# Two-layer expert routing in two equal halves, each with its own counts and slots, nine early tiles instead of eleven

## What is computed

```
x = x + 0.5 * ffn(layernorm(x), router, experts, shared)      # layer 1
x = x + attn(layernorm(x))                                    # test-time training, 1024 steps in order
x = x + 0.5 * ffn(layernorm(x), router, experts, shared)      # layer 2

def ffn(h):
    probs = softmax(h @ router.T)            # 8 experts
    p, i = top_k(probs, 2)
    w = p / sum(p)
    out = sum over k of w[k] * (relu(h @ fc[i[k]].T) ** 2 @ proj[i[k]].T)
    return out + relu(h @ shared_fc.T) ** 2 @ shared_proj.T
```

## Time and profile before

| what | us |
|---|---|
| median of 3 runs | 483.91 |
| lowest and highest run | 483.69, 485.36 |
| span of the profiled execution | 483.5 |
| PE busy in it | 433.4 (90%) |
| DVE busy | 280.3 (58%) |
| ACT busy | 244.4 (51%) |
| POOL busy | 242.4 (50%) |

### The profile page before, as it was taken

One profiled execution on the slowest core, in us unless ns is written; L12 is line 12 of the kernel. 1 busy time (PEld: TensorE's weight loads), 2 busy tenths in 40 slices (PEclk: granted clock), 3 DMA queues, 4 the chain that ended last, 5 costly groups with the idle time before them and its releaser, 6 DMA issues.

```text
span 483.5 us, 9868 instructions
## 1 busy us (share of the span) xinstructions
PE 433.4 (90%) x2875; PEld 356.7 (74%) x2875; DVE 280.3 (58%) x1031; ACT 244.4 (51%) x617; POOL 242.4 (50%) x371
## 2 busy tenths in 40 slices
PE   7899899999918889999999999989999699999940
PEld 5444599999903668999999999974644399999930
DVE  3836445555429657677777767754965245555514
ACT  2495255555510545655556555544597145555520
POOL 4367777445510344455555646542247767454530
PEclk9599999999976999999999999999799999999975
DMA  8981435100055300000000000000001417110028
GB/s 223 253 290 50 111 89 172 31 28 28 12 155 170 82 1 1 1 2 2 1 3 0 1 2 2 3 1 0 2 23 55 112 50 204 35 34 28 20 62 216
DMA packets 34513, 30.89 MB, mean 64 GB/s; under 512 B 3838, under 2 KB 30085, under 8 KB 34464
## 3 DMA queue, kind: packets, MB, share of 16 engines
q1 hardware_dynamic: 24608, 19.17, 14.8%
q0 software_dynamic: 4544, 8.47, 5.4%
q10 hardware_dynamic: 5312, 2.62, 2.1%
HBM read 15.55 MB, written 15.61 MB: 64 GB/s over the span
## 4 chain that ended last, share of the span: by engine, by line
PE 80%; DVE 5%; DMA 5%; POOL 4%; issue 3%; ACT 1%; ACTq 0%; DVEq 0%; SPq 0%; POOLq 0%
PE bank L1307 17%; PE bank L741 15%; PE bank L728 14%; PE bank L689 5%; PE bank L699 3%; PE bank L599 3%; POOL slots_dram L1436 3%; DMA stage<-y_dram 3%; PE bank L1101 2%; PE bank L716 2%; PE bank L1176 2%; PE bank L1139 1%; PE bank L1161 1%; PE bank L1205 1%; DVE stats L419 1%
## 5 line engine op out<-in xcount | busy, mean ns | idle before, releaser
L1693 DVE TENSOR_TENSOR sq<-bank,relu 128x512 f32<-128x512 f32 x86 | 59.4, 691 | 85.6 <-ACT relu L839 85.3
L1441 POOL DMA_INDIRECT y_dram<-y_out,stage x78 | 76.5, 981 | 60.8 <-ACT y_out L865 54.3
L741 PE MATMUL bank<-proj_w,sq 128*128 x624 | 86.4, 281 | 2.9 <-DVE sq L1693 2.9
L728 PE MATMUL bank<-tileT,tile_w 128*128 128x128 f32 x624 | 83.2, 277 | 0.1
L1436 POOL DMA_INDIRECT slots_dram<-rows,slots x64 | 63.0, 984 | 37.4 <-issue 15.5
L741 PEld LDWEIGHTS bank<-proj_w,sq 128*128 128x128 f32 x624 | 75.6, 191 | 6.5 <-issue 3.6
L839 ACT ACTIVATE relu<-bank 128x512 f32<-128x512 f32 x94 | 56.0, 596 | 47.5 <-PE bank L728 38.0
L728 PEld LDWEIGHTS bank<-tileT,tile_w 128*128 128x128 f32 x624 | 76.9, 194 | 0.4 <-ACT tileT L831 0.4
L865 ACT ACTIVATE y_out<-bank,stage 128x128 f32<-128x128 f32 x78 | 28.6, 367 | 33.3 <-PE bank L741 33.3
L1302 POOL TENSOR_TENSOR sq<-sq,last_rows 128x128 f32<-128x128 f32 x32 | 14.6, 456 | 53.6 <-DVE sq L1278 53.6
L689 PE MATMUL bank<-ln_t,fc_w 128*128 128x512 f32 x64 | 36.9, 678 | 0.0
(11 more groups left out here) (280 smaller groups left out, 1035.3 us busy)
## 6 DMA issues: line engine op xcount, KB each, us to landing
slots_dram<-pad SPq DMA_DIRECT2D x2, 2535.0 KB, 14.1
stage<-slots_dram SPq DMA_DIRECT2D x18, 260.0 KB, 4.7
fc_w<-experts SPq DMA_DIRECT2D x1, 2048.0 KB, 20.9
proj_w<-experts SPq DMA_DIRECT2D x1, 2048.0 KB, 23.8
stage<-y_dram SPq DMA_DIRECT2D x8, 256.0 KB, 5.5
stage<-y_dram ACTq DMA_DIRECT2D x8, 256.0 KB, 6.1
y_dram<-y_out,stage POOLq DMA_INDIRECT x78, 2.3
res<-x SPq DMA_DIRECT2D x4, 256.0 KB, 4.2
```

What stands on the lines that cost most here:

```text
L728: last = nc.tensor.matmul(bank[i % 2][:, f_cols], tile_w[:, i % 2, f_cols], tileT[:, (f * NQ + tile_q(i)) % 2, tile_cols(i)], start=True, ...
L741: last = nc.tensor.matmul(bank[4 + i % 2][:, 0:P], sq[:, i % 2, f_cols], proj_w[:, k, f_cols], start=j == 0, stop=j == FJ - 1)
L1441: nc.gpsimd.indirect_dma_start(y_dram.ap(), bass.IndirectOffsetOnAxis(tiles[:, t, P:P + 1].bitcast(U32), 0), y_out[:, t % YBUFS, :], None, ...
L1693: nc.vector.tensor_tensor(wide_of(i)[2], wide_of(i)[0][:], wide_of(i)[1], ALU.mult)\
```

## The change

`HALF` becomes 8 blocks, so 16 scatters belong to each half, and `EARLY` becomes 9 tiles. The whole of the routing is done once for each half: `choose` (two best experts, counts), `weigh` and `weights_made` (the two weights), then `first_slots` for the first half and `late_slots` for the second, whose counts take a second set of products on PE (`pe_counts(pe, f, 1)`). The second half's norms, its 1/sqrt (now on DVE, `late_scale`) and its logits come after the first half's slots. The words are made last. Tiles now fall into three kinds (full and mixed tiles of the first half, late tiles), and lie in memory in the reverse order. The first three loads are of three tiles each, then four, and two at the end. `ahead_of` and `word_at` are as before.

```diff
-HALF = NBLK // 2 + 1
+HALF = NBLK // 2
 EARLY = HALF * TOPK - E + 1
-YBUFS = EARLY + 1
-FIRST = EARLY % GRP
-NQ = (NT - FIRST + 2 * GRP - 1) // GRP
+YBUFS = 12
+GROUP_STARTS = (*range(0, EARLY, 3), *range(EARLY, NT, GRP), NT)
+NQ = len(GROUP_STARTS) - 1
-ROWS_FIRST = (6, 2)
-COUNT_AT = 2
+ROWS_FIRST = (5, 3)
+RATIO_AT = (-1, 1)
+LATE_RATIO_AT = (6, 7)
+RATIO_AFTER = 2
+COUNTS_AT = ((-1, 6), (3, 7))
+LATE_LOGITS_AT = 4
...
+        def late_scale(dve, at):
+            b = of_half(1)
+            y, z, x = rs_y[:, b], rs_t[:, b], rs_x[:, b]
+            for _ in range(3):
+                dve_link(dve, nc.vector.tensor_tensor(z, x, y, ALU.mult), at)
+                dve_link(dve, nc.vector.scalar_tensor_tensor(z, z, -0.5, y, ALU.mult, ALU.mult), at)
+                dve_link(dve, nc.vector.scalar_tensor_tensor(y, z, 1.5, y, ALU.add, ALU.mult), at)
+            nc.vector.scalar_tensor_tensor(shift[:, b], mv[:, b, 0], -1.0, y, ALU.mult, ALU.mult).then_inc(rstd_done, 1)
...
-        def pe_counts(pe, f):
+        def pe_counts(pe, f, h):
-            pe.wait_ge(upto_done, f + 1)
+            pe.wait_ge(upto_done, 2 * f + h + 1)
+            if h:
+                pe.wait_ge(slots_done, 2 * f + h)
...
+            return i > NS and i - NS + 3 in GROUP_STARTS[2:NQ]
...
-                if f and i == COUNT_AT:
-                    pe_counts(pe, f)
+                for h in range(2):
+                    if i == COUNTS_AT[f][h]:
+                        pe_counts(pe, f, h)
+                if f and i in RAW_AT:
+                    pe_raw_columns(pe, f, RAW_AT[i])
+                if f and i == LATE_LOGITS_AT:
+                    for g in range(HG, NG):
+                        pe_logits(pe, f, g)
...
+            def routed_late(f):
+                late_scale(dve, at)
+                choose(dve, at, f, 1)
+                weigh(dve, at, f, 1)
+                weights_made(dve, at, f, 1)
+                late_slots(dve, at, f)
+                experts_of_tiles(dve, at)
...
-            layer_norm()
-            route(dve, at, 0)
+            dve.wait_ge(x_in[0], 16 * B)
+            norms_of_pair(0)
+            norm_guess(dve, at, 0)
+            dve.wait_ge(x_in[1], 16 * B)
+            norms_of(2)
+            choose(dve, at, 0, 0)
+            weigh(dve, at, 0, 0)
+            weights_made(dve, at, 0, 0)
+            first_slots(dve, at, 0)
+            norms_of(3)
+            norm_guess(dve, at, 1)
+            routed_late(0)
             tiles_of(0)
...
+            choose(dve, at, 1, 0)
+            weigh(dve, at, 1, 0)
+            weights_made(dve, at, 1, 0)
+            first_slots(dve, at, 1)
+            dve.wait_ge(res_done, NG + 4)
+            norms_of_pair(2)
+            norm_guess(dve, at, 1)
+            routed_late(1)
             tiles_of(1)
```

More of the change, by code:

```diff
@@ L470, in normalise, with choose @@
                                         ALU.subtract, ALU.mult).then_inc(ln_done, 1)
[L472 to L484, removed]
+        def choose(dve, at, f, h):
+            b = of_half(h)
+            n4 = [P, TOPK, HALF, E]
+            dve.wait_ge(logits_done, 2 * f + h + 1)
+            dve_link(dve, nc.vector.tensor_copy(logits[:, b, :].rearrange("p b e -> p (b e)"),
+                                                bank[6 - h][:, b.start * E:b.stop * E]), at)
+            for n in range(b.start, b.stop):
+                last = nc.vector.max(top[:, n, :], logits[:, n, :])
@@ L485, in route @@
             dve_link(dve, last, at)
[L486 to L489, removed]
+            for n in range(b.start, b.stop):
+                last = nc.vector.max_index(topi[:, n, :], top[:, n, :], logits[:, n, :])
@@ L490, in route @@
+            dve_link(dve, last, at)
+            dve_link(dve, nc.vector.tensor_copy(topif[:, b], topi[:, b, 0:TOPK]), at)
             dve_link(dve, nc.vector.tensor_tensor(
[L491 to L494, removed]
@@ L511, in route, with first_slots @@
+        mixed, full, begun = n_tiles[:, 0, :], n_tiles[:, 1, :], n_tiles[:, 2, :]
+        late_from, mixed_at, full_at = (bounds[:, n * E:(n + 1) * E] for n in range(3))
+        def first_slots(dve, at, f):
+            dve.wait_ge(counted, 2 * f + 1)
+            dve_link(dve, nc.vector.tensor_tensor(
+                reached[:], counts_of(0).unsqueeze(2).unsqueeze(3).to_broadcast([P, E, 2, HALF]), fill_steps[:],
+                ALU.is_gt), at)
             dve_link(dve, nc.vector.tensor_reduce(n_tiles[:, 1:3, :].rearrange("p h e -> p e h"), reached[:], AX.X,
@@ L518, in route @@
[L518 to L547, removed]
+                first_sums[:, 1:2 * E + 1], ones[:, 0:2 * E], n_tiles[:, 0:2, :].rearrange("p h e -> p (h e)"), 0.0,
+                ALU.mult, ALU.add), at)
+            dve_link(dve, nc.vector.tensor_scalar(bounds[:, E:3 * E + 1], first_sums[:], first_sums[:, 2 * E:2 * E + 1],
+                                                  float(NT), ALU.subtract, ALU.add), at)
```

293 lines of the change are left out of this document (183 added, 110 removed).

## The result

The changed kernel takes 509.73 us (median of 4 runs, 508.11 to 516.74), against 483.8 for the kernel before in the same series. The ratio is 1.0514, with a 95% interval of 1.0481 to 1.0547: 25.9 us slower, where 20.7 were forecast, and at the upper end of the range of 490 to 510. The ratio leaves out runs that are over 1.5% above the fastest of their kernel (here 516.74), while the medians keep them. The profiled execution spans 508.3 us, 24.8 more than that of before. Each run's time lies some 2 us above its span (510.05 and 508.3 here), so the traced execution of before, 483.5 us long, belongs to the run of 485.36 and not to the median one, as the 0.4 us named ahead of the prediction would have it.

What follows compares the result with a forecast made beforehand. PE, with 80% of the chain, was taken to bound the kernel, the words having little slack. 2.5 + 1.9 + 3.6 in layer 1 and 7.2 + 1.9 + 3.6 in layer 2 made 20.7 us: 504.5 us, range 490 to 510.

Steps and rivals of the forecast that it cites:

- the rival of cheaper operations: DVE's small operations cheaper at half size, the late half 4 us less per layer; about 495.5 us, chance 0.14.
- Layer 1, the words: DVE casts the words at 38.2; PE's sixth shared projection stands at 38.25 against 35.73, +2.5 us.
- Layer 2, the words: Words at 372.4, 11.7 behind the projection's old time; 4.5 replace the first load's wait, net +7.2 us.
- The clock: PE runs at half clock behind each wait for the words, +1.9 us in each layer.
- The late tiles: PE waits for the first late group's load, landing at T0 (first routed fc products) + 17.3; 3.6 us per layer.
- The rival of a second fall of the clock: The late load's waits drop PE's clock once more, 1.9 us again in each layer; 508.3 us, chance 0.14.
- The other side, words in time: Second half's DVE work done before PE's step 8, only the 32 scatters bind; 481.6 to 485 us, chance 0.12.

Runs made afterwards that it cites:

- the run with the late group moved: Changed kernel with the first late tiles (9 to 12) transposed behind the ninth tile's fc products, not the sixth tile's projection: 502.55 us, 1.0384.
- last combined kernel: Changed kernel with later word loads, counts, late-tile transposes and layer 2 shared-row transposes, 14 squares on ACT, scatters untied from PE: 481.83 us, 0.994.
- half fillers: Changed kernel with filler products on PE ahead of the words' wait, 6 in layer 1, 3 and 4 in layer 2: 504.13 us, 1.0408.

## Why the prediction was right

The direction, the mechanisms (PE waits for the words, for the clock behind that wait, and for the late tiles) and their places were right; the sum was 4.1 us short in the profiled execution (20.7 for 24.8). The stated 498 to 508 for all terms at their bounds is too narrow: the bounds add up to 13.1 and 28.1 us, 497 to 512, and 509.73 lies inside that. Likewise the rival of cheaper operations adds up to 496.1, not 495.5.

- **Layer 1, the words.** Forecast: cast at 38.2, the projection at 38.25, +2.5. Measured: cast at 39.14, projection at 40.21, +4.5. The first half's slots were 1.3 us later than worked out (21.69 for 20.35), because DVE stood for the counts from PE, which ran at half clock from 12 to 20 us:

```profile
18.15 0.29 DVE L583 TENSOR_TENSOR reached<-bank,fill_steps 128x128 f32<-128x128 f32 x1 [1.39 <-PE bank L704]
```

That belongs to the execution and not to the kernel. In the trace of the run with the late group moved, whose lists on DVE, ACT and PE are the same up to T0, the clock was back at 1.00 by 15 us, the counts came without a wait, the slots were cast at 20.21 and the words at 37.16. There PE's wait is in two parts, 2.51 us at the second half's count products and 2.52 at the words, and T0 is at 60.83, where the forecast had it (61) and not at 63.83:

```profile
20.21 0.17 DVE L574 CAST slots<-slot_f 128x16 uint32<-128x16 f32 x1
...
37.16 0.16 DVE L631 CAST words<-word_f 1x5 int32<-1x5 f32 x1
...
60.83 2.05 PE L809 MATMUL bank<-tileT,tile_w 128*128 128x128 f32 x16 [0.24 <-ACT tileT L926]
```

A difference of up to 3 us at T0 of layer 1 between two traces is therefore no sign of an edit. Besides, between the end of the cast and PE's projection lie 0.9 us (0.7 in layer 2), which the forecast put at nothing. The trace of before could not show this: the words were long there when PE came.
- **Layer 2, the words.** Less the 9.53 us of layer 1, the words were cast at 370.9 (forecast 372.4), the projection came at 371.7, and T0 at 395.5, 9.4 us later than before (forecast 7.2 and 1.9 of clock, 9.1). That this total fits is in part luck: the projection was 0.7 early and the clock took 1.0 more than forecast. What was not forecast is the split: PE stood 3.11 us already at the second half's count products, and 4.59 at the words.
- **The clock.** This term of the sum was mis-sized: 1.9 forecast in each layer, 2.7 and 2.9 measured (from the projection to T0 23.62 and 23.76 us, for 20.9 before and 20.9 with the wait filled). The half clock lasted about 5.4 us behind the 6.27 idle, not the 3.8 seen behind 3.54.
- **The late tiles.** Forecast 3.6 in each layer; measured 1.77 idle in layer 1 and 4.10 in layer 2. The last scatter was where it was put, 10.4 us after T0; the landing was not the same 6.9 behind it but 5.2 (74.25 to 79.41) and 7.3 (415.46 to 422.77). The rival of a second fall of the clock came true in layer 2 alone. From T0 on, layer 1 lost 2.3 us (9.53 - 7.22) and layer 2 5.9 (24.8 - 9.5 - 9.4). Their sum, 8.2 for the forecast's 7.2, is near only because one was too small and the other too large.
- **The rivals.** Cheaper small operations fell: the linked operations of the new 1/sqrt ran 0.20 us apart, as before. The other side, words in time, was wrong for this kernel. The sentence cited for it (the Trainium skill, "Perfetto Trace Analysis", section "Optimizing Scalar/DVE Operations") says that breaking up instructions may let work be completed sooner. Here that was so for the first part (slots 3.6 us sooner) and not for the last (words 10.1 later), and PE waited for the last. The last combined kernel took 481.83, inside the 481.6 to 485 of that rival, but not by its way: its words are cast at 36.88 and 374.96, not before 33 and 362; their consumers were moved behind them.

Not settled: why the late load landed 2 us faster behind the last scatter in layer 1 than in layer 2, and which of its edits bring the last combined kernel below the kernel before, rather than level with it.

## What to carry to other kernels

Splitting a serial piece of work to get its first result early made its last result later here (3.6 us sooner, 10.1 later); before splitting, list every consumer of that last result on every engine, and what stands behind the producer in its own list. Here the words, DVE's squares and DVE's additions were three such things, one under the other, and each showed only when the one above it was gone. A releaser named by the trace is the one that came last; where an edit that removes it alone changes nothing, another wait was binding. And a run that lands on the expected time has not yet shown the expected reason: the half fillers gave the 504 us that were asked for, mostly in another place.

## What the runs showed of the hardware

A wait of PE can cost more than its idle time. Behind the two waits for the words (6.27 and 4.59 us) PE ran at half clock, and the same work up to T0 took 2.7 and 2.9 us longer (23.62 and 23.76 us for 20.9). Filler products that kept PE busy through the wait brought it back to 20.9 in both layers without any useful work; fillers that left 3.03 us idle in layer 2 did not (22.45).

The idle time of 1.77 us left the clock up and those of 3.03, 4.10 and 6.27 were followed by half clock. In between it went both ways: 2.31 us idle ahead of the late group's transposes were followed by half clock in layer 1 of the run with the words' loads moved (0.50 in the second microsecond behind), and not in layer 2 of the run with half the fillers (1.00 throughout). So a wait near 2 us can't be priced by its length alone.
